# Cross-attention and fp4 feed-forward: norm, fp4 scaling, residual adds and a split moved to GpSimd, and the piece order drawn across groups

## The reference

```
x = x + attention(layernorm(x), ctx) @ Wo + bo      # 16 heads of 16, softmax(Q K^T / 4) V
n = layernorm(x)
h = silu(fp4(n) @ fp4(w_gate)^T) * (fp4(n) @ fp4(w_up)^T)   # 704 wide
x = x + fp4(h) @ fp4(w_down)^T
```

## Time and profile before

| | us |
|---|---|
| median of three runs | 3553.26 |
| profiled execution, its own time | 3561.53 |
| its span on the core | 3559.8 |
| TensorE busy | 3335.2 (94%) |
| VectorE busy | 2874.6 (81%) |
| ScalarE busy | 2254.1 (63%) |
| GpSimd busy | 696.0 (20%) |
| mean granted TensorE clock | 0.945 of full speed |

### The profile page before, as it was taken

One profiled execution on the slowest core, in us unless ns is written; L12 is line 12 of the kernel. 1 busy time (PEld: TensorE's weight loads), 2 busy tenths in 40 slices (PEclk: granted clock), 3 DMA queues, 4 the chain that ended last, 5 costly groups with the idle time before them and its releaser, 6 DMA issues.

```text
span 3559.8 us, 55150 instructions
## 1 busy us (share of the span) xinstructions
PE 3335.2 (94%) x19606; PEld 1692.0 (48%) x19606; DVE 2874.6 (81%) x6429; ACT 2254.1 (63%) x4512; POOL 696.0 (20%) x796
## 2 busy tenths in 40 slices
PE   7999999999999999999999999999999999999996
PEld 4344544544445454544544444454544544445444
DVE  6877888887887888888887887978888887887865
ACT  2666667666666666667666666666666666666662
POOL 0212112212111122112212111122111121111122
PEclk6898999999999999999999999999999999999998
DMA  4232123232223222133232222322133231232200
GB/s 89 53 51 48 34 54 53 34 67 34 44 47 50 51 44 46 35 56 54 34 67 31 44 47 45 57 45 46 34 57 53 35 66 24 47 53 36 42 19 8
DMA packets 120777, 163.24 MB, mean 46 GB/s; under 512 B 47125, under 2 KB 93606, under 8 KB 120506
## 3 DMA queue, kind: packets, MB, share of 16 engines
q1 hardware_dynamic: 120506, 159.73, 25.7%
HBM read 46.22 MB, written 8.39 MB: 15 GB/s over the span
## 4 chain that ended last, share of the span: by engine, by line
PE 79%; DVE 11%; ACT 4%; SPq 2%; DMA 2%; issue 1%; POOL 0%; DVEq 0%; POOLq 0%
PE out_ps L990 19%; PE ring L1004 15%; PE ring L977 15%; PE ring L940 7%; DVE piece_max L1336 6%; PE ring L951 5%; PE ring L915 4%; PE ring L907 4%; ACT probs L1106 3%; PE ring L931 2%; SPq L796 2%; PE ring L948 2%; DMA q_stack<-neg_rows 2%; PE ring L925 1%; PE ring L896 1%
## 5 line engine op out<-in xcount | busy, mean ns | idle before, releaser
L1336 DVE TENSOR_REDUCE piece_max<-ring 128x1 f32<-128x402 f32 x4096 | 2069.7, 567 | 303.2 <-PE ring L1004 291.2
L1106 ACT ACTIVATE probs<-ring 128x512 f32<-128x512 f32 (+1 forms) x3328 | 1794.6, 600 | 696.7 <-PE ring L977 677.8
L1004 PE MATMUL ring<-k_stack,q_stack 48*128 48x402 f32 x4096 | 886.0, 406 | 50.6 <-DVE piece_max L1336 34.0
L990 PE MATMUL out_ps<-probs,v_ones 128*17 128x512 f32 x6656 | 921.3, 627 | 1.4 <-ACT probs L1106 1.4
L977 PE MATMUL ring<-q_stack,k_stack 50*128 50x512 f32 (+1 forms) x3328 | 844.9, 474 | 46.9 <-DMA q_stack<-neg_rows 36.2
L977 PEld LDWEIGHTS ring<-q_stack,k_stack 50*128 50x128 f32 (+1 forms) x3328 | 350.7, 187 | 881.0 <-issue 277.3
L1004 PEld LDWEIGHTS ring<-k_stack,q_stack 48*128 48x128 f32 x4096 | 468.9, 196 | 321.3 <-DVE piece_max L1336 177.6
L1384 POOL TENSOR_TENSOR h<-h,h_grid 128x704 f32<-128x704 f32 (+1 forms) x68 | 101.3, 1489 | 1176.2 <-DVE h_grid L1169 1176.2
L940 PE MATMUL ring<-wgu_T,xq_T 128*128 128x512 f32 (+1 forms) x1080 | 250.4, 383 | 1.8
L990 PEld LDWEIGHTS out_ps<-probs,v_ones 128*17 128x17 f32 x6656 | 111.4, 96 | 233.9 <-issue 199.8
L940 PEld LDWEIGHTS ring<-wgu_T,xq_T 128*128 128x128 f32 x1080 | 193.9, 188 | 52.5 <-issue 21.4
(11 more groups left out here) (159 smaller groups left out, 2521.2 us busy)
## 6 DMA issues: line engine op xcount, KB each, us to landing
k_stack<-k_parts SPq DMA_DIRECT2D x256, 200.1 KB, 4.5
k_stack<-k_parts SPq DMA_DIRECT2D x256, 100.1 KB, 4.3
ctx_in<-in_ctx SPq DMA_DIRECT2D x47, 384.0 KB, 3.9
q_stack<-q_parts SPq DMA_DIRECT2D x256, 64.0 KB, 2.3
x_in<-in_x SPq DMA_DIRECT2D x16, 512.0 KB, 5.5
q_stack<-q_parts SPq DMA_DIRECT2D x256, 32.0 KB, 2.0
resid<-in_x SPq DMA_DIRECT2D x62, 128.0 KB, 2.7
out<-x SPq DMA_DIRECT2D x62, 128.0 KB, 1.7
```

Source lines behind the costliest of these rows:

```text
L990: last = pe.matmul(out_ps[32 * j:32 * j + V1, :], v_ones[0:r, batch % 2, m, PER_GROUP * g + j, :], probs[0:r, step % 2, j, :], start=(m == ...
L1004: pe.matmul(ring[:, bank(kind, batch, item), 0:PW], q_stack[rows, at, t * P:(t + 1) * P], k_stack[rows, at, a:b], start=True, stop=True).t ...
L1106: act.activation(probs[0:r, step % 2, j:j + n, :], ring[0:r, at:at + n, :], ACT.Exp, scale=SCORE_SCALE).then_inc(probs_ready, n)
L1336: dve.tensor_reduce(piece_max[:, j:j + many, t, c], ring[:, at:at + many, 0:PW], AX_X, ALU.max).then_inc(pieces_max, many)
```

## The change

In the bodies (not in the tail, and `ln1_apply` not in the lead-in), GpSimd takes over from VectorE: `ln1_apply` and `ln2_apply` (it first negates the mean, then adds and multiplies), the scaling of xq and of h (two instructions each: by the constant, then by the blocks' inverse), the two residual adds, and the low part of xq_T. GpSimd doesn't read PSUM here, so ScalarE copies out_proj into `x1`, down into a new tile `down_out`, and the transposed xq a second time, into `heads_T`. `ready` names the semaphore by which the others wait for GpSimd's results.

The pieces are no longer bound to "next group in this group": their order runs on, six pieces (`EARLY_PIECES` pairs) of a group being ready before the group ahead of it begins, and steps 11 and 12 hold pieces too, of the group after the next once those of the next are through. `piece_max` gets two halves. The order within a step is a list for each step; in step 11 the events stand behind S23. The half steps of the lists change. `probs` is addressed by slot, eight as before. Code for merged pieces, which was switched off, goes.

```diff
+EARLY_PIECES = 3
-STEP_ORDER = "S01 P W01 P S23 P V"
+STEP_ORDERS = ['P S01 W P S23 P V', 'S01 P W P S23 P V', 'S01 P W S23 P V', 'S01 P W P S23 P V', 'S01 P W P S23 P V', 'S01 P W P S23 P V', 'S01 P W P S23 P V', 'S01 P W P S23 P V', 'S01 P W P S23 P V', 'S01 P W S23 P V', 'S01 P W P S23 P V', 'S01 P P S23 W P V', 'S01 P S23 P V']
 POST_AT = [
-    [4, 5, 5, 9, 13, 14, 19, 20, 20, 21, 23, 23, 23, 26, 33, 34, 38],
-    [22, 23, 23, 23, 32, 37, 38, 43, 45, 45, 48, 48, 51, 51, 56, 62, 65],
-    [52, 55, 55, 58, 59, 59, 65, 66, 66, 66, 68, 69, 70, 73, 78, 80, 85],
-    [74, 74, 74, 74, 74, 78, 82, 86, 86, 87, 87, 93, 95, 95, 100, 101, 102],
+    [5, 9, 12, 13, 14, 16, 19, 21, 22, 22, 22, 26, 30, 31, 39, 39, 40],
+    [20, 22, 22, 24, 32, 36, 40, 43, 48, 48, 48, 48, 49, 52, 60, 62, 65],
+    [54, 57, 57, 58, 58, 60, 64, 66, 66, 66, 67, 67, 68, 74, 80, 80, 97],
+    [65, 67, 68, 75, 79, 81, 85, 86, 86, 86, 88, 91, 96, 96, 100, 101, 103],
 ]
-OWN_AT = [6, 13, 14, 17, 18]
-PRE_AT = [26, 28, 29, 30, 37, 37, 47, 48, 51, 51, 54, 55, 59, 62, 66, 69, 69, 70, 78, 83, 87, 91]
+OWN_AT = [6, 15, 15, 16, 18]
+PRE_AT = [24, 27, 27, 30, 45, 45, 50, 56, 61, 61, 63, 66, 69, 69, 70, 71, 71, 72, 74, 76, 85, 99]
-STACK0_AT = [17, 71]
-LN1 = 6
+STACK0_AT = [18, 70]
+LN1 = 8
 PIECES_AT = [
-    [3, 3, 4, 3, 2, 3, 3, 3, 3, 3, 2, 0, 0],
-    [3, 3, 3, 2, 3, 3, 4, 3, 3, 3, 2, 0, 0],
-    [3, 3, 3, 2, 3, 3, 3, 3, 3, 3, 3, 0, 0],
-    [3, 3, 4, 4, 4, 1, 3, 3, 2, 3, 2, 0, 0],
+    [3, 3, 3, 4, 1, 1, 1, 4, 3, 3, 3, 0, 2],
+    [4, 2, 1, 2, 3, 1, 3, 4, 4, 2, 3, 1, 1],
+    [1, 2, 3, 1, 2, 3, 3, 4, 4, 3, 4, 1, 3],
+    [3, 3, 2, 4, 4, 1, 1, 3, 3, 4, 3, 0, 1],
 ]
...
+    def by_pool(kind, event):
+        return kind != "tail" and event[0] in ("out_proj", "down", "xq_T")
+    def ready(kind, batch, event):
+        if not by_pool(kind, event):
+            return drained(kind, batch, event)
+        return {"xq_T": xq_low, "out_proj": x1_ready, "down": x1_done}[event[0]], count(batch - 1, QT, event[1] + 1)
...
+        of, n = 1, 2 * EARLY_PIECES
         for g in range(PHASES):
...
+                            if kind != "last" or of < PHASES:
+                                put(0, "piece", of, n)
+                            of, n = of + (n + 1) // NPIECE, (n + 1) % NPIECE
...
# ScalarE
+                    if kind != "tail" and (event[1] or old):
+                        act.wait_ge(xq_low, count(old, QT, event[1]))
                     act.copy(quarter(kind, event[1]).heads_T, work[:, 0:D].rearrange("p (k t) -> p k t", k=2)).then_inc(this_drained, 1)
+                elif name == "out_proj":
+                    t = event[1]
+                    act.wait_ge(x1_free[t % 2], count(old, 32, 32 + 16 * (t // 2)))
+                    act.copy(x1_of(kind, t), work[:, 0:D]).then_inc(this_drained, 1)
+                elif name == "down":
+                    if event[1] or old:
+                        act.wait_ge(x1_done, count(old, QT, event[1]))
+                    act.copy(down_out[:], work[:, 0:D]).then_inc(this_drained, 1)
+                elif name == "xq_T" and by_pool(kind, event):
+                    act.copy(xq_T[:, 0], work[:, 0:D].rearrange("p (k t) -> p k t", k=2))
+                    act.copy(heads_T[:], work[:, 0:D].rearrange("p (k t) -> p k t", k=2)).then_inc(this_drained, 1)
...
# GpSimd
+            def fp4_scale(src, inverse, done, base):
+                pool.wait_ge(done, base(3))
+                pool.tensor_scalar(src, src, BELOW_TIE, 1.0, ALU.mult, ALU.mult).then_inc(scaled, 1)
+                pool.wait_ge(scaled, scale_number[0])
+                scale_number[0] += 1
+                pool.tensor_tensor(fp4_blocks(src), fp4_blocks(src), over_block(inverse, src.shape[1] // BLOCK), ALU.mult).then_inc(done, 1)
...
+                    pool.tensor_scalar(mean_var[:, :, 0], mean_var[:, :, 0], -1.0, 1.0, ALU.mult, ALU.mult).then_inc(ln1_neg, 1)
...
+                        last = pool.tensor_scalar(x_in[:, t, :], x_in[:, t, :], mean_var[:, t, 0:1], rstd[:, t:t + 1], ALU.add, ALU.mult)
...
+                    pool.tensor_tensor(x1_of(kind, t), x1_of(kind, t), resid_of(kind, t), ALU.add).then_inc(x1_ready, 1)
...
+                    pool.tensor_tensor(x1_of(kind, t), x1_of(kind, t), down_out[:], ALU.add).then_inc(x1_done, 1)
...
+                    pool.tensor_tensor(xq_T[:, 1], heads_T[:], xq_T[:, 0].bitcast(F32), ALU.subtract).then_inc(xq_low, 1)
...
+                    pool.tensor_scalar(q.mean_var[:, 0:1], q.mean_var[:, 0:1], -1.0, 1.0, ALU.mult, ALU.mult).then_inc(ln2_neg, 1)
...
+                    pool.tensor_scalar(q.xq, x1_of(kind, t), q.mean_var[:, 0:1], q.rstd, ALU.add, ALU.mult).then_inc(ln2_step, 1)
...
```

More of the change, by code:

```diff
@@ L258, in build, with ring_of @@
     BANKS = sum(RINGS)
-    RING_OF = {"scores": RING_FOR[0], "piece": RING_FOR[1], "round": RING_FOR[2]}
+    def ring_of(kind, item):
+        return RING_FOR[0 if item[0] == "scores" else 1 if item[0] == "piece" else 3 if by_vector(kind, item[1]) else 2]
+    VALUES_LEFT = STEPS
+    for step in range(STEPS):
+        ready = step - (STEPS - VALUES_LEFT)
+        VALUES_LEFT -= min(STEP_ORDERS[step % KEY_TILES].split().count("V"), ready)
     def transposes(event):
@@ L302, in spread @@
                 done += cost
-                while n < NPIECE and done * NPIECE >= total * (n + 1):
-                    new.append((("piece", group, n), 0))
+                while n < many and done * many >= total * (n + 1):
+                    new.append((("piece", group + n // NPIECE, n % NPIECE), 0))
                     n += 1
@@ L326, in sequence, with put_events @@
             return seq
+        value = 0 if kind == "first" else -VALUES_LEFT
+        pending = sorted(EVENTS[kind].items())
+        def put_events(until):
+            while pending and pending[0][0] <= until:
+                for e in pending.pop(0)[1]:
+                    put(0, "event", e)
+                    put_rounds([e])
+        of, n = 1, 2 * EARLY_PIECES
         for g in range(PHASES):
-            ahead = g < PHASES - 1 or kind != "last"
-            n = 0
             for m in range(KEY_TILES):
                 step = g * KEY_TILES + m
-                left, slots = ahead * 2 * PIECES_AT[g][m], STEP_ORDER.count("P")
-                for what in STEP_ORDER.split():
+                left, slots = 2 * PIECES_AT[g][m], STEP_ORDERS[m].count("P")
+                for what in STEP_ORDERS[m].split():
                     if what == "P":
@@ L343, in sequence @@
                             put(NQ, "scores", step, int(j))
[L344 to L350, removed]
+                    elif what == "W":
+                        put_events(2 * step + 1)
+                    elif value < step:
+                        put(4 * NQ, "weighted", value)
+                        value += 1
+        put_events(2 * STEPS)
         return seq
@@ L430, in bank_user @@
         return kind, batch, BANK_USERS[kind][of][n]
[L432 to L447, removed]
     ctx = ExitStack()
@@ L560, in build @@
         ctx_hi = sem("ctx_hi")
+        xq_low = sem("xq_low")
+        x1_ready = sem("x1_ready")
+        x1_done = sem("x1_done")
         prep_hi = sem("prep_hi")
@@ L1033, in handle @@
                     return
-                if name not in ROUNDS or name in ("out_proj", "down", "heads_out"):
+                if name not in ROUNDS or name == "heads_out" or name in ("out_proj", "down") and not by_pool(kind, event):
                     return
@@ L1265, in handle @@
                     dve.bn_aggr(q.mean_var, q.stats).then_inc(ln2_step, 1)
-                elif name == "ln2_apply":
+                elif name == "ln2_apply" and kind == "tail":
                     t = event[1]
@@ L1394, in handle @@
                 name = event[0]
-                if name in ("ln2_stats", "xq_scale", "h_grid"):
+                if name in ("ln2_stats", "ln2_apply", "xq_max", "xq_scale", "h_scale", "h_grid"):
                     q = quarter(kind, event[1])
```

144 lines of the change are left out of this document (88 added, 56 removed), and 8 rows, old and new, of the table TAIL_AT.

## The result

| | before, us | after, us |
|---|---|---|
| median | 3555.28 (4 runs) | 3376.14 (4 runs, 3374.22 to 3380.50) |
| profiled execution | 3561.53 | 3376.89 |
| its span | 3559.8 | 3375.1 |

The ratio is 0.9492 with a 95% interval of 0.9469 to 0.9515: 5.1% faster, 179 us. The forecast was faster, by 72 us, and its range ended at 3400 us.

The account below looks back on a forecast made before the run. TensorE, busy 94% of the span, was taken as the bound, with 147 us idle and 124 us of low clock in the body. Idle -39 and clock -33 gave -72: 3489.5 us from 3561.5, range 3400 to 3575.

Parts of the forecast that it names:

- a: TensorE's wait for ScalarE's heads_T: more half steps before out_proj take 22 of 25.1 us off.
- b: TensorE's wait for neg_parts: maxima in step 11 standing behind S23 takes 12 us off.
- c: TensorE's wait for q_stack at a group's end: pieces before the first scores and in step 12, 5 us off.
- d: TensorE's waits for VectorE's backlog (piece maxima, ctx_T), 54 us: half goes, 27 off; range 54 off to 0.
- e: Tile 3's xq_T to gate_up has one half step for its ScalarE and GpSimd chain: 7 us on.
- f: Early pieces in step 12 need k_stack sooner: TensorE stands 2.3 us there, 20 us on in all.
- the clock: TensorE's low-clock loss in the body, 124 us, falls in proportion to idle time: 33 us off.
- Rival 1: VectorE stands behind GpSimd at ln2_stats, xq_max and the grids, making the kernel slower: 3613 us, chance 0.15.
- Rival 2: More GpSimd work slows VectorE through shared SBUF interfaces, 50 us of VectorE's time: 3495 us, chance 0.08.
- Rival 3: TensorE's waits pass to ScalarE, which has 68 us more work; 10 to 15 us gained: 3540 us, chance 0.16.
- Rival 4: The clock comes back wholly: idle -70 and clock -90 us, 3393 us, chance 0.13.
- Rival 5: Early pieces fail as k_stack lands 4 us late in each body, 60 us instead of 20: 3555 us, chance 0.06.

Follow-up runs that it names:

- e16: Before, with heads_T of tiles 0, 1 and 3 one or two half steps earlier and nothing else: 3586.12 us (ratio to before 1.0076).
- e13: After, with the events of step 11 (max_parts and maxima) ahead of S23 again: 3353.30 us (ratio to before 0.9431).
- e6: After, with the next batch's q_proj and first k_proj, and the copies to k_stack, brought forward: 3350.80 us (ratio to before 0.9435).
- e9: After, with the pieces of steps 11 and 12 and the early ones moved into steps 0 to 10: 3547.60 us (ratio to before 0.9983).
- e11: e9, with the four score matmuls of step 12 done twice: 3521.35 us (ratio to before 0.9909).
- e12: Before, with the four score matmuls of step 12 done twice: 3527.79 us (ratio to before 0.9919).
- e4: After, with the pieces and the step order of before: 3567.26 us (ratio to before 1.0031).
- e7: After, with 480 further VectorE reductions whose results nobody uses: 3440.97 us (ratio to before 0.9693).
- e1: After, with all seven moved pieces of work back on VectorE and no extra ScalarE copies: 3458.66 us (ratio to before 0.9719).
- e2: After's moved work on GpSimd and ScalarE, with the lists, pieces and step order of before: 3495.65 us (ratio to before 0.9824).
- e8: Before, with 600 further GpSimd adds whose results nobody uses: 3590.65 us (ratio to before 1.0113).

## Why the prediction was wrong

**Direction and engine times were right.** VectorE 2698 us (2671 forecast), GpSimd 1097 (1100), ScalarE without a new bound.

**The steps, one by one** (TensorE's idle time in the body, forecast and measured). a, heads_T: 22 off, 25 off; but e16 shows that the distance by itself only moves this wait to others and makes the kernel slower; it is a gain with the lists as a whole. b, neg_parts: 12 off, 6.6 off (17.0 to 6.2, and 4.2 of new waits for ScalarE), and wrong as an edit: e13. c, q_stack: 5 off, 4.5 off. d, VectorE's backlog: 27 off, 49 off (54 to 2.9, and 2.2 at L972); only its far end had that. e, xq_T of tile 3: 7 on, nothing. f, k_stack: 20 on, 27.2 on, 14 waits of 1.9 us where 2.3 us were reckoned; the 1 us that I took off for covering the next wait was not there, as e6 shows. The sum was 39 off; in the body it is 61 (146.7 to 85.2), over the whole span 59. So the idle term was too small as well, by 20, and that is d.

**The step that failed is the clock, and with it the sum's form.** "33 off", in proportion to the idle time, was 77. e9, e11 and e12 show that it doesn't follow the sum of idle time: e9 has 18 us more of it than after (183.6 against 165.5) and loses 155 us more to the clock, and e12 wins clock by work that is of no use. What weighs most is what stands at the ends of the 64 groups, where the earlier trace rows showed the low clock; the prediction read that row and then spread the clock over all waits alike. The traces bear this out: of the stretches at the lower level that begin in the body, 37 of 40 before, all 18 after and 40 of 51 in e9 begin between 10 us ahead of the issue of the four neg_rows DMAs and 12 us behind it, while a group lasts some 50. It is not all: in e4 18 of 41 begin elsewhere. The pieces in steps 11 and 12, which it priced under c and d at some microseconds, are the change's dearest part as long as the rest is as it is.

**A term was missing.** 49 us of the gain lie inside TensorE's "busy" time. I took 147 us idle and 124 us of clock as all that could be won in the body. e7 shows that there is more: loading VectorE slows the kernel by a third of the load, and more than a third of that is in no idle row. e1 and e2 show that neither the order (8 us) nor the engines (25 us the other way) bring the 49 by themselves; what TensorE does with that time stays open.

**The rivals.** Rival 1 (VectorE stands behind GpSimd) did not come: 20 us of waits; in e2, with the old half steps, it did, with 150 us, and even there did not make the kernel slower. Rival 2 (contention) is real in e8, 52 us of VectorE's time; here the instructions that stayed are longer by 7 us in sum. Rival 3: ScalarE holds TensorE 6 us longer at group_out and before `maxima`, no more. Rival 4 (idle -70, clock -90: 3393) was nearest in both terms, 59 and 77; with the rest of 49 the time falls below even that, and below the range. Rival 5's wait was there, at the forecast's size.

## What to carry to other kernels

Where TensorE's granted clock is under full, look first at what stands right ahead of each low stretch and put work there, if only by moving it: having 18 of a body's 256 pieces there, and the early ones with them, was worth 171 us, and even useless matmuls paid, as long as the clock was low. A list of waits isn't a list of gains: price an engine beside the bound by loading it (a third of its time, here), since part of the price shows in no wait of the bound. An order fitted by hand or by search is worth something only whole; take its parts back one at a time before you believe in one.

## What the hardware showed that I had not expected

- 256 matmuls more (some 31 us of work by the rows) made the kernel faster, twice: 28 us on before (clock 0.945 to 0.961) and 26 us on e9 (0.923 to 0.935).
- With equal busy times on VectorE, ScalarE and GpSimd within 0.5%, after and e9 differ by 171 us.
- GpSimd's multiply by a constant of 128x704 takes 0.78 us, the product of two inputs 1.39 us. On VectorE the scale in one instruction took 0.89 us.
